# One message-passing layer on a graph, one core: VectorE makes the product of the second layer and the picked rows before the older unit's places, bucket sum and row numbers

## The reference, cut to what matters

```python
h    = relu(layernorm(x)) @ W_in2f.T                    # 12500 x 128
Wij  = smu(attr @ W_f1.T + b_f1) @ W_f2.T + b_f2        # 400000 x 128
x_ij = h[dst] * (Wij * edge_weight[:, None])            # rows of h picked per edge
agg  = segment_sum(x_ij, src)                           # 12500 x 128
out  = x + smu(agg @ W_o1.T + b_o1) @ W_o2.T + b_o2
```

## Time and profile before

| | |
|---|---|
| median of 3 runs | 4155.02 us (4153.83 to 4162.68) |
| the profiled execution | 4145.66 us, its span 4143.9 us |
| PE busy | 3504.1 us (85%) |
| DVE busy | 3785.0 us (91%) |
| ACT busy | 2194.0 us (53%) |
| POOL busy | 3050.2 us (74%) |
| DMA | 736.87 MB, mean 178 GB/s |
| mean granted clock of TensorE | 0.981 of full speed |

### The profile page before, as it was taken

The page is one execution under the profiler, slowest core; times in us unless marked ns, Lnnn a source line. Parts: engine busy times, 40 slices in busy tenths (PEclk is TensorE's granted clock), DMA queues, the critical chain, the costliest instruction groups (busy, mean ns, idle before and its releaser), DMA issues.

```text
span 4143.9 us, 90305 instructions
## 1 busy us (share of the span) xinstructions
PE 3504.1 (85%) x19070; PEld 2324.8 (56%) x19070; DVE 3785.0 (91%) x13416; ACT 2194.0 (53%) x7302; POOL 3050.2 (74%) x3173
## 2 busy tenths in 40 slices
PE   6677768888888888888888899988889989998889
PEld 2344335555555555555555566665556666665658
DVE  8889779998999889999899999999999999999997
ACT  4677555555555555555555555555555545455543
POOL 4777777777777777777777777777777767777772
PEclk9999999999999999999999999999999999999999
DMA  7566656666666555665555666666656776765658
GB/s 210 151 172 186 166 146 182 189 188 187 186 172 163 163 161 159 166 164 162 159 160 164 174 187 191 189 187 176 168 167 184 202 189 196 204 190 169 182 163 237
DMA packets 459534, 736.87 MB, mean 178 GB/s; under 512 B 87168, under 2 KB 255466, under 8 KB 459104
## 3 DMA queue, kind: packets, MB, share of 16 engines
q1 hardware_dynamic: 291606, 461.44, 44.7%
q0 software_dynamic: 100000, 206.60, 14.4%
q10 hardware_dynamic: 67626, 65.48, 4.8%
HBM read 465.36 MB, written 267.82 MB: 177 GB/s over the span
## 4 chain that ended last, share of the span: by engine, by line
POOL 25%; DVE 23%; issue 20%; DMA 14%; PE 13%; ACT 2%; ACTq 1%; POOLq 1%; DVEq 0%; SPq 0%
POOL sorted_rows L590 25%; DMA sorted_rows<-msg,row_idx 14%; DVE product L1012 5%; DVE seg_hot L1038 4%; DVE hg L1004 3%; PE p_w L1219 3%; DVE act L981 3%; DVE onehot L990 3%; PE p_seg L1264 3%; PE p_h L1234 2%; PE p_m L1225 2%; PE p_z L1214 1%; DVE pair_hot L996 1%; DVE pick L985 1%; DVE row_idx L1023 1%
## 5 line engine op out<-in xcount | busy, mean ns | idle before, releaser
L590 POOL DMA_INDIRECT sorted_rows<-msg,row_idx x3125 | 3009.3, 963 | 1017.1 <-issue 913.8
L725 ACT ACTIVATE msg<-p_m,weight 128x128 f32<-128x128 f32 x3136 | 896.2, 369 | 1136.2 <-PE p_m L1225 1121.4
L1264 PEld LDWEIGHTS p_seg<-seg_hot,seg 128*128 128x128 f32 x8288 | 1028.4, 192 | 323.4 <-issue 321.6
L1264 PE MATMUL p_seg<-seg_hot,seg 128*128 128x112 f32 x8288 | 1027.5, 274 | 15.0 <-issue 8.1
L1225 PE MATMUL p_m<-ident,hg 128*128 128x128 f32 x3136 | 516.5, 288 | 571.6 <-DVE hg L1004 568.1
L1012 DVE CUSTOM_DVE_ANT_0 product<-onehot,p_pos,start_at 128x112 bf16<-128x112 bf16 x3136 | 853.0, 328 | 9.1 <-PE p_pos L1253 4.3
L1219 PE MATMUL p_w<-act,w_f 128*128 128x512 f32 x1568 | 828.9, 611 | 4.2 <-DVE act L981 4.2
L1214 PE MATMUL p_z<-attr,w_f 128*128 128x512 f32 x1568 | 819.5, 605 | 14.3 <-DMA attr<-in_attrT 9.4
L1225 PEld LDWEIGHTS p_m<-ident,hg 128*128 128x128 f32 x3136 | 339.7, 143 | 796.5 <-DVE hg L1004 646.9
L709 ACT ACTIVATE gelu<-p_z 128x512 f32<-128x512 f32 x784 | 469.3, 599 | 460.4 <-PE p_z L1214 455.8
L1234 PE MATMUL p_h<-pick,win 128*128 128x512 bf16 x2352 | 654.4, 388 | 1.1 <-DMA win<-h 1.1
(11 more groups left out here) (116 smaller groups left out, 2242.3 us busy)
## 6 DMA issues: line engine op xcount, KB each, us to landing
seg<-sorted_rows SPq DMA_DIRECT2D x448, 322.5 KB
seg<-sorted_rows SPq DMA_DIRECT2D x196, 516.0 KB
ends<-ends SPq DMA_DIRECT2D x392, 256.0 KB
sorted_rows<-msg,row_idx POOLq DMA_INDIRECT x3125
sorted_rows<-zero_rows ACTq DMA_DIRECT2D x336, 129.0 KB
win<-h SPq DMA_DIRECT2D x392, 96.0 KB
attr<-in_attrT SPq DMA_DIRECT2D x392, 80.0 KB
seg<-sorted_rows SPq DMA_DIRECT2D x56, 387.0 KB
```

The lines of the kernel that those rows point to most:

```text
L590: pool.indirect_dma_start(out=sorted_rows[:, :], out_offset=bass.IndirectOffsetOnAxis(ap=row_idx[:, slot, k:k + 1], axis=0), in_=msg[:, sl ...
L725: last = act.activation(msg[:, slot, k, 0:F], p_m[:, k, :], ACT.Copy, scale=weight[:, bass.ds(n.value(TILES_U, k), 1)])
L1264: last = pe.matmul(out, seg[:, it.slot, l * it.tiles + k, 0:F], seg_hot[:, it.slot, l * it.tiles + k, :], start=(k == 0), stop=(k == it.ti ...
```

## The change

In VectorE's `step`, `product_of` of the older unit moves from behind `row_numbers` to the front of the older unit's works. Its waits move with it. No instruction is added or taken away.

```diff
                 if st.has(1):
+                    product_of(st.at(1), st.v(1))
                     places(st.at(1), st.v(1), st.ring(1), st.i is None and st.rnd == 0 and st.c == mid_step + 1)
                 for it in st.items(1):
                     if it.closes:
                         gather_sum(it)
                 if st.has(1):
                     row_numbers(st.at(1), st.v(1), st.ring(1))
-                    product_of(st.at(1), st.v(1))
```

## The result

The changed kernel takes 4189.27 us (median of 5 runs, 4184.60 to 4204.78); the kernel before, run beside it, 4157.99 (5 runs, 4153.83 to 4163.40). The ratio is 1.0080, 95% interval [1.0067, 1.0093]: slower by 31 us, where 4154 in a range of 4142 to 4169 was forecast. The profiled executions lie 43.6 us apart (span 4187.5 after, 4143.9 before), because the profiled execution of before (4145.66) was quicker than any of its five runs here.

A forecast was written before the change was run, and what follows sets the result against it. The prediction took POOL's scatters, 1.263 us apart, as the bound. Its terms, -2 + 1 + 0 = -1 on the profiled 4145.66, with the median's 9.4 us difference carried over, gave 4154 us, range 4142 to 4169.

The forecast's parts named there:

- The bound: Whole kernel: POOL's scatters, 1.263 us from start to start, set the pace; reordering VectorE wins at most 47 us.
- Product earlier: Ordinary and two-load beats: p_w ends 0.6 us earlier, the work queued behind the product 0.7 us later; cost 0.
- rival B: Two-load beats: TensorE does not come earlier, the product waits 0.4 us in 48 beats; +19 us, 4174, chance 0.05.
- TensorE comes to that beat almost 1 us earlier: Two-load beats: p_m, no longer held by the product, lets TensorE arrive earlier; taken as 0, bad end 19 us.
- a new one for places in front of rank: Sign expected in the new profile: TensorE waits for places before rank, its product wait in p_m all but gone.
- The landing wait behind the product: VectorE's row_idx wait: POOL's slack against late landings grows by about 1 us; -2 us, ends 0 and -6.
- some 200: Sign expected in the new profile: row_idx still waits some 200 us for landings, with the product ahead of them.
- rival D: VectorE's landing waits were the bound after all, some 60 of 205.6 us go; 4095, chance 0.01.
- Openings: Nine later rounds' first beats: the product waits for p_w, +1.7 us each on VectorE, mostly covered; with 3412 and 3627 stalls +1.
- rival A: Nine round openings: the product's wait for p_w is nowhere given back; +13 us, 4168, chance 0.10.
- Its sign of being wrong: POOL's scatter count from 3408 well under 158 in 209 us would show the bare openings.
- Start: First scatters: about 1.2 us won at one stall is lost at the next; 0, ends 0 and -1.2.

The follow-up runs named there:

- k2: Kernel before with the product first only in rounds 4 and 7, at the usual pace: 4170.57 us, beside 4162.90 for the kernel before on its chip.
- k1: Kernel before with the product first in round 0 alone, at the usual pace: 4182.25 us, beside 4162.90 for the kernel before on its chip.
- e1: Kernel before with the product first in round 0 alone, at the slower pace; mean of three such runs 0.0003 over the kernel before.
- f2: Same edit as e1 (product first in round 0 alone), run again at the slower pace; mean of the three such runs 0.0003 over the kernel before.
- g4: Same edit as e1 (product first in round 0 alone), run once more at the slower pace; mean of the three such runs 0.0003 over the kernel before.
- g1: The changed kernel itself, unchanged, run at the slower pace: ratio 1.0133 to the kernel before.
- h3: The kernel before, unchanged, run again for a second trace; it met the usual pace: 4148.33 us.
- the f runs: A group of follow-up runs at the slower pace, mostly with the product first in some rounds or beats only; the kernel before took 5232 us there.
- the k runs: Three follow-up runs at the usual pace: product first in round 0, in rounds 4 and 7, and changed kernel with some sums moved; 4182.25, 4170.57, 4180.92 us.

## Why the prediction was wrong

**The bound.** Right in the rounds up to 6, where POOL is at 1.263 us between stalls after as before. In round 7 it was not POOL: the beat was at 5.23 us before the change, with VectorE 98% busy, so each wait on VectorE counted in full. "It can lose more, if it makes VectorE's beat longer than 5.05 us" is what happened in rounds 0 and 7.

**Product earlier: the step that failed.** The sentence was "Queued behind the product on VectorE are places, bucket sum and row numbers, 0.7 us later than now; of these only places have a near follower, rank, and it is in this sum. Cost 0." The bucket sum has a near follower too: TensorE's p_seg, where two loads come in a beat or in the one before, which stands in front of everything that TensorE does for the product. The earlier trace rows had a beat of two loads, and its p_seg appeared in the text as TensorE time only, never as a waiter for VectorE. Measured: TensorE waits 24.2 us in 21 times for the sum, the product 17.8 us in 20 times for the hg that comes late by it, and round 7 is 21 us longer (24 in k2).

**The bad end of that step, rival B.** It put the trouble in two-load beats and priced it at 19 us, 4174, with a chance of 0.05. The place was right for round 7 and the size near by luck: the mechanism was another (a wait for p_w of 0.4 us in 48 beats), and so was the count. Round 4, with 29 of those 48 beats, lost 1 us. Its loads come in pairs for one sum, so that even two of them close one sum at most, and its trace shows no wait of p_seg for a sum. The 13 beats of round 7 and the 3 at the start of round 8 close two. The cost was 1.6 us for each of the 13, in place of 0.4 for each of 48.

**"TensorE comes to that beat almost 1 us earlier".** True in ordinary beats, false behind a late sum: TensorE's wait for the product in p_m fell from 568.1 us to 109.2, and part of what was won there was given to places in front of rank and, in round 7, to the sum:

```profile
PE p_pos L1239 <- DVE place L1012: 206.7, 491, 0.4
...
PE p_m L1225 <- DVE hg L1004: 109.2, 135, 2.7
```

The first of these was foretold ("a new one for places in front of rank"), and, at most 0.4 us long, it went with no loss in rounds 1 to 6.

**The product's other input.** The whole walk treated p_w as the product's last input and never hg. The kernel before already showed that wait in its page:

```profile
L1004 DVE SCALAR_TENSOR_TENSOR hg<-p_w,bias_w,hg 128x512 f32<-128x512 f32 x784 | 586.5, 748 | 18.8 <-ACT hg L719 10.4
```

After the change it is 62.3 us in 75 times in place of 10.4 in 17: 36.0 of it in round 0, where ScalarE has the node work, and 17.8 in round 7. Round 0 is the second missing term, 16 to 20 us in the changed kernel and 24 to 27 in k1.

**The landing wait behind the product: -2.** Not to be told apart. The wait fell to 142.6 from 205.6 us (I had said "some 200"), and rounds 1 to 6 did not gain. There it fell from 161.1 to 108.0, and 17 us more of waiting for p_w and 39 in front of seg_hot (L1038) came in its place; this bought nothing, since POOL was the pace: the point made against rival D holds. ScalarE's own wait for landings (L713) grew from 162.9 to 472.0 us, also without a cost in those rounds.

**Openings: +1.** Right but for details. The product waits for p_w behind the counts as walked, 2.0 to 3.5 us in each of the nine, and the stall went to the next scatter unit:

```profile
3432.63 0.25 DVE L1030 SCALAR_TENSOR_TENSOR counts<-p_pos,seed_row 1x112 f32<-1x112 f32 x1
...
3434.84 0.75 DVE L1004 SCALAR_TENSOR_TENSOR hg<-p_w,bias_w,hg 128x512 f32<-128x512 f32 x1 [1.95 <-PE p_w L1219]
3435.65 0.95 POOL L590 DMA_INDIRECT sorted_rows<-msg,row_idx  x1 [9.46 <-PE p_w L1219]
```

9.46 against 7.01 and 1.09 in two units before is about 1.4 us more, where the walk had 0.35 less. Rounds 1 to 6 with six openings lost 1 us, so rival A (+13) is out. Its sign of being wrong was met all the same: POOL starts 141 scatters in the first 209 us of round 7 in place of 158. That count sees a loss in round 7, whatever its cause.

**Start: 0.** Slightly off. The two stalls near the start took 5.30 and 5.45 us in place of 4.78 and 3.45; the later scatter starts at 63.69 in place of 61.15, 2.5 us that are part of round 0's 16.

In sum -2 + 1 + 0 = -1 stands against about +5 for what it priced (1 in rounds 1 to 6, 1.4 at the opening of round 7, 2.5 at the start). Two waits that it did not look up, some 20 us in round 7 and 14 to 18 in round 0 with the start left out, made the result.

## What to carry to other kernels

When an instruction moves ahead of others in an engine's queue, list for each one that it passes who waits for it on every engine, in the rare beats too, and list all inputs of the one moved, with the latest of them in each stage. If a passed result is needed by an engine in front of an input of the moved one, the move closes a ring: the late result comes back as a wait of the engine on which the move was made. On an engine that is 98% busy this costs its length each time that the rare beat comes. Of the orders tried here, none was faster than that of the kernel before, in which what frees another engine's buffer stands ahead of the product and the product, which waits for most, goes last.

## What the runs showed that I had not expected

- The same kernels have a second pace. The kernel before took 4148 to 4163 us in some sessions and 5170 to 5232 in others. In those, traces of the same kernel differ by up to 0.2 us per beat in round 7 (6.74 to 6.96 in e1, f2 and g4), so single rounds tell effects of 10 us, not of 3. TensorE's granted clock is lower in the traces of the slow pace, 0.87 to 0.90 in the mean against 0.97 to 0.99 (1.00 is 2.4 GHz, 0.50 is 1.2), so its own instructions are not alike: a matmul of p_w has 717 ns in g1 and 614 in h3. In g1 TensorE's results reach their waiters late:

```profile
2011.45 0.96 POOL L590 DMA_INDIRECT sorted_rows<-msg,row_idx  x1 [0.30 <-issue]
2014.34 1.14 ACT L725 ACTIVATE msg<-p_m,weight 128x128 f32<-128x128 f32 x4 [6.16 <-remote]
2015.16 0.95 POOL L590 DMA_INDIRECT sorted_rows<-msg,row_idx  x1 [2.75 <-remote]
```

  Idle stretches of TensorE over 3 us number 141 in g1 and 11 in the trace of before at 4148 us. In rounds 1 to 3 most of them recur every four beats, which is one pass of the hardware loop. Their cause stays open. The number of the chip does not tell the pace: the f runs and the k runs both have number 7, with 5232 and 4163 us for the kernel before.
- A stall of TensorE can cost twice. In k1 the granted clock is 1.00 from 242 to 244 and 0.50 from 246 to 248; in the four microseconds between 242 and 246 TensorE had 0.94 us of matmuls. The two matmuls of p_w at 248.38 then take 1.91 us in place of 1.02:

```profile
242.00:244.00 2.00, 0.81 (x2) 0.00 (x0) 0.53 (x3) 1.61 (x6) 1.65 (x2) 1.00 0.97 259
244.00:246.00 2.00, 0.13 (x1) 0.13 (x2) 0.94 (x4) 1.81 (x7) 1.43 (x2) 0.75 0.50 170
246.00:248.00 2.00, 2.00 (x9) 1.09 (x10) 1.86 (x11) 0.00 (x0) 1.45 (x2) 0.50 0.11 33
```

  (stretch, us, busy time of PE, PEld, DVE, ACT, POOL with counts, granted clock, DMA share, GB/s.) From 200 to 440 the mean is 0.90 in k1, 0.97 in the changed kernel, and 0.97 and 0.99 in the two traces of before. The low clock in k1 may be why its round 0 lost more than the changed kernel's; that was not tested.
